# Work shared out anew between ScalarE and VectorE, and four expert lists loaded into other buffers, in a two-layer convolution and expert kernel

## The reference, cut to what matters

```python
# layer 0: grouped convolution, then a mixture of experts
c0 = conv(x, weight(32, 8, 9), groups=4, padding=4) + ctx[:, :, None] + bias[None, :, None]
logits = c0 @ W_gate + b_gate                        # 8 experts
_, top_idx = top_k(logits, 2)                        # 2 experts for each of the 4096 rows
x = x + mean_of_2(relu(c0 @ W_e[top] + b_e[top]))
# layer 1: convolution kernels mixed by attention, then an int4 product
att = softmax(gelu(gelu(cond @ W0 + b0) @ W1 + b1) @ W2 + b2)
c1 = einsum('boi,bih->boh', einsum('bk,koi->boi', att, weight), x) + (att @ bias_k)[:, :, None]
x = x + (c1 @ dequant(qweight, scales, zeros) + bias)
```

## Time and profile before

| | us |
|---|---|
| median of 3 runs | 516.99 (516.94 to 518.96) |
| the profiled execution's own time | 518.35 |
| its span in the profile | 516.6 |
| TensorE busy in that span | 491.2 (95%) |
| VectorE busy | 345.6 (67%) |
| ScalarE busy | 197.6 (38%) |

### The profile page before, as it was taken

One profiled execution on the slowest core, in us unless ns is written; L12 is line 12 of the kernel. 1 busy time (PEld: TensorE's weight loads), 2 busy tenths in 40 slices (PEclk: granted clock), 3 DMA queues, 4 the chain that ended last, 5 costly groups with the idle time before them and its releaser, 6 DMA issues. The chain is left out here.

```text
span 516.6 us, 10152 instructions
## 1 busy us (share of the span) xinstructions
PE 491.2 (95%) x2284; PEld 321.6 (62%) x2285; DVE 345.6 (67%) x1087; ACT 197.6 (38%) x341; POOL 157.5 (30%) x178
## 2 busy tenths in 40 slices
PE   5999999999869999999999999999997999999996
PEld 5999999989844443444444444444544777777674
DVE  6877888877546657573354435453445799999996
ACT  6798999999721111111111111111222222222220
POOL 9154555444435522233323332333224000000000
PEclk9999999999969999999999999999997999999998
DMA  6569878998467686676666657575554688889852
GB/s 182 142 233 298 285 241 269 361 374 269 154 165 188 209 228 168 165 201 181 174 187 163 183 150 197 163 191 146 155 143 169 245 292 292 277 292 287 286 184 102
DMA packets 90050, 110.94 MB, mean 215 GB/s; under 512 B 25198, under 2 KB 61726, under 8 KB 88980
## 3 DMA queue, kind: packets, MB, share of 16 engines
q1 hardware_dynamic: 71808, 69.14, 47.1%
q0 software_dynamic: 11664, 36.24, 19.7%
q10 hardware_dynamic: 6536, 5.09, 3.3%
HBM read 65.44 MB, written 46.51 MB: 217 GB/s over the span
## 5 line engine op out<-in xcount | busy, mean ns | idle before, releaser
L1213 PE MATMUL bank<-we,lT 128*128 x536 | 233.7, 597 | 0.7 <-DVE ring_a L953 0.7
L1213 PEld LDWEIGHTS bank<-we,lT 128*128 128x128 f32 x536 | 101.8, 191 | 128.1 <-issue 127.9
L539 POOL DMA_INDIRECT pairs_d<-ring_b,pair_i x71 | 71.0, 999 | 161.0 <-DVE pair_i L942 109.2
L630 ACT ACTIVATE ring_b<-ring_a 128x512 f32<-128x512 f32 x71 | 44.7, 630 | 196.3 <-DVE ring_a L953 188.2
L953 DVE TENSOR_TENSOR ring_a<-bank,be_bc 128x512 f32<-128x512 f32 x71 | 49.0, 691 | 101.8 <-PE bank L1213 92.4
L1187 PE MATMUL bank<-wconv,phases 128*128 128x128 f32 x768 | 93.8, 280 | 1.2 <-ACT phases L367 1.2
L522 POOL DMA_INDIRECT lists_d<-token_list,row_i x64 | 66.7, 1042 | 83.3 <-ACT token_list L596 57.1
L1187 PEld LDWEIGHTS bank<-wconv,phases 128*128 128x128 f32 x768 | 90.8, 196 | 1.4 <-ACT phases L367 1.4
L367 ACT COPY phases<-xt 32x512 f32<-32x512 f32 x64 | 71.4, 1116 | 1.2
L939 DVE STREAM_TRANSPOSE lT<-xt 128x512 f32<-128x512 f32 x71 | 49.9, 703 | 11.1 <-DMA keys<-lists_d 10.8
L367 DVE COPY phases<-xt 32x512 f32<-32x512 f32 x64 | 44.7, 698 | 10.2 <-PE bank L1187 8.5
(11 more groups left out here) (196 smaller groups left out, 384.3 us busy)
## 6 DMA issues: line engine op xcount, KB each, us to landing
xt<-lists_d SPq DMA_DIRECT2D x284, 64.0 KB, 2.1
xt<-in_x SPq DMA_DIRECT2D x60, 256.0 KB, 3.9
we<-pairs_d SPq DMA_DIRECT2D x28, 512.0 KB, 4.8
we<-in_L_ffn_W_e SPq DMA_DIRECT2D x8, 1024.0 KB, 6.5
out<-orow_list SPq DMA_DIRECT2D x32, 256.0 KB, 2.8
lists_d<-orow_list SPq DMA_DIRECT2D x8, 257.0 KB
be_bc<-in_L_ffn_b_e ACTq DMA_DIRECT2D x4, 512.0 KB, 9.5
words<-pairs_d POOLq DMA_DIRECT2D x4, 512.0 KB, 5.3
```

The costliest lines, as they stand in the source:

```text
L539: pool.indirect_dma_start(pairs_d, bass.IndirectOffsetOnAxis(ap=pair_i[:, s % DR:s % DR + 1], axis=0), ring_b[:, s % U, :], None, bounds_c ...
L630: act.activation(ring_b[:, j, :], ring_a[:, j % 2, :], ACT.Relu, scale=0.5).then_inc(result_ready, 1)
L1213: mm = pe.matmul(ps_exp[j % 2][:, :], lT[:, j, p * P:(p + 1) * P], we[:, bass.ds(expert, 1), p, :].rearrange("m a n -> m (a n)"), start=(p ...
```

## The change

There are four edits.

1. Phase 2 is copied by ScalarE for the groups with an even number only. For the odd ones it is copied by VectorE (`split_third`), at the end of the step, behind `chosen`; `dve_split` is then counted by that copy. For group 1 it stands right behind the two other copies at the start.
2. The lists of slots 0 to 3 are loaded into `ring_a[0]`, `ring_a[1]`, `ring_b[2]` and `ring_b[3]` and not into `xt`, and no longer wait for the last x to be copied. Slot 4, the first in `xt`, waits for that now.
3. The three products for the mixing kernels stand in front of `gate_and_rows` of group 31, not behind `count_ranks` of group 31.
4. `warm_up` is called twice more at the start: four transposes in front of those of the convolution's weights, and eight behind them.

```diff
@@ -121,6 +121,7 @@
         token_list = sb("token_list", [P, U, LK])
         htok = token_list[:, :, 0:L]
         ring_b = sb("ring_b", [P, U, L])
+        first_list = [ring_a[:, 0, :], ring_a[:, 1, :], ring_b[:, 2, :], ring_b[:, 3, :]]
         orow_list = sb("orow_list", [P, 2, LK])
         orow = orow_list[:, :, 0:L]
         ident = sb("ident", [P, P])
@@ -362,6 +363,10 @@
                 ins.then_inc(taps_ready, 1)
 
 
+        def list_of(a, ja):
+
+            return first_list[a] if isinstance(a, int) and a < len(first_list) else xt[:, ja, :]
+
         def split_phase(copy, q, jq, jb):
 
             return copy(phases[q * C:(q + 1) * C, jb, :, 1:P + 1],
@@ -421,15 +426,15 @@
                     else:
                         sp.reg_load(row_reg, tab[0:1, bass.ds(a - EARLY, 1)])
                     row = sp.snap(row_reg, min_val=0, max_val=E * REGION - P)
-                    if isinstance(a, int) and a < XR:
+                    if isinstance(a, int) and a == XR:
                         sp.wait_ge(act_split, NG)
                         sp.wait_ge(dve_split, NG)
-                    else:
+                    if not isinstance(a, int) or a >= XR:
                         wait(sp, lT_ready, a - XR + 1)
                         wait(sp, pair_ready, a - XR + 1)
 
                     for mh in range(MH):
-                        sp.dma_start(xt[mh * B:(mh + 1) * B, ja, :].rearrange("r (h n) -> r h n", h=MH),
+                        sp.dma_start(list_of(a, ja)[mh * B:(mh + 1) * B, :].rearrange("r (h n) -> r h n", h=MH),
                                      lists_d[bass.ds(row, P), mh * P:(mh + 1) * P].rearrange("(h r) n -> r h n", r=B)
                                      ).then_inc(list_in[ja], 16)
                     sp.dma_start(keys[:, ja, :], lists_d[bass.ds(row, P), L:LK]).then_inc(list_in[ja], 16)
@@ -573,9 +578,9 @@
                     ja = (j + 2) % U
                     wait(act, x_in[ja], ring_count(a, ja, XR))
                     wait(act, conv_done, a - 1)
-                    for q in range(PH // 2, PH):
-                        ins = split_phase(act.copy, q, ja, j % 2)
-                    ins.then_inc(act_split, 1)
+                    if ja % 2 == 0:
+                        split_phase(act.copy, 2, ja, j % 2)
+                    split_phase(act.copy, 3, ja, j % 2).then_inc(act_split, 1)
                 b = g - 2
                 if live(b, NG):
                     jb = (j - 2) % U
@@ -700,9 +705,15 @@
 
                 wait(dve, x_in[ja], ring_count(a, ja, XR))
                 wait(dve, conv_done, a - 1)
-                for q in range(PH // 2):
-                    ins = split_phase(dve.tensor_copy, q, ja, ja % 2)
-                ins.then_inc(dve_split, 1)
+                split_phase(dve.tensor_copy, 0, ja, ja % 2)
+                ins = split_phase(dve.tensor_copy, 1, ja, ja % 2)
+                if ja % 2 == 0:
+                    ins.then_inc(dve_split, 1)
+
+            def split_third(ja):
+
+                if ja % 2 == 1:
+                    split_phase(dve.tensor_copy, 2, ja, ja % 2).then_inc(dve_split, 1)
 
             dve.memset(wfull[:, :, :], 0.0).then_inc(wfull_zero, 1)
 
@@ -777,6 +788,7 @@
                 deq_step(dve.scalar_tensor_tensor(terms_w[:, :], full_low, odd[0:RK, 0:1], full, ALU.mult, ALU.add))
 
             split_x(1, 1)
+            split_third(1)
             dve.wait_ge(consts, N_CONSTS)
 
             def context_columns():
@@ -870,6 +882,8 @@
                     wait(dve, chosen1_ready, a + 1)
                     wait(dve, rank_done, a - 3)
                     dve.scalar_tensor_tensor(chosen[:, ja, :], iota_e[:, :], e2, chosen1[:, :], ALU.is_equal, ALU.add).then_inc(chosen_ready, 1)
+                if live(g + 2, NG):
+                    split_third((j + 2) % U)
 
             n_early = [0]
 
@@ -937,7 +951,7 @@
                 wait(dve, list_in[ja], (a - ja) * (80 // XR) + 80)
                 wait(dve, exp_done, a - AHEAD + 1)
                 dve.transpose(lT[:, ja, :].rearrange("m (p h r) -> m h p r", p=PH, h=MH),
-                              xt[:, ja, :].rearrange("r (h p l) -> r h p l", h=MH, p=PH)).then_inc(lT_ready, 1)
+                              list_of(a, ja).rearrange("r (h p l) -> r h p l", h=MH, p=PH)).then_inc(lT_ready, 1)
                 wait(dve, result_out[ja], 16 * ((a - DR - ja) // U + 1))
                 dve.scalar_tensor_tensor(pair_i[:, a % DR:a % DR + 1], keys[:, ja, 1:2], slot_expert[:, a:a + 1],
                                          keys[:, ja, 0:1], ALU.not_equal, ALU.add).then_inc(pair_ready, 1)
@@ -1113,7 +1127,7 @@
             pe.wait_ge(cond_in, 32)
             pe.transpose(ps_misc[:, 0:N], cond_sb[:, :], ident[:, :]).then_inc(condT_done, 1)
             pe.transpose(ps_misc[:, N:N + C], cw_sb[:, :], ident[0:C, 0:C]).then_inc(condT_done, 1)
-
+            warm_up(WARM_START // 2)
             for t in range(SHIFTS):
                 pe.wait_ge(dve_taps, t + 1)
                 pe.wait_ge(act_taps, t + 1)
@@ -1121,6 +1135,7 @@
                     mm = pe.transpose(ps_w[t][:, p * C:(p + 1) * C],
                                       wsel[:, t * PH + p, :, :].rearrange("o q i -> o (q i)"), ident[0:C, 0:C])
                 mm.then_inc(wT_done, 1)
+            warm_up(WARM_START)
 
             def context_products():
 
@@ -1235,6 +1250,7 @@
                         mm = pe.matmul(ps_low[0][0:RK, :], ones_r[:, :], wq[:, q, :], start=(q == 0), stop=(q == 3))
                     mm.then_inc(colsum_done, 1)
 
+            mix_layers(NG + 1 - mlp_first)
             gate_and_rows(NG - 1, (NG - 1) % U)
             pe.wait_ge(early, N_EARLY)
             pe.wait_ge(we_in, 16 * E)
@@ -1242,7 +1258,6 @@
             count_ranks(NG - 2, (NG - 2) % U)
             product(1, 1)
             count_ranks(NG - 1, (NG - 1) % U)
-            mix_layers(NG + 1 - mlp_first)
             for s in range(2, 5):
                 product(s, s % U)
             pe.wait_ge(tab_ready, 1)
```

## The result

The changed kernel takes **511.34 us** (median of 4 runs, 510.92 to 512.60) against 517.19 for the kernel before beside it (4 runs, 516.94 to 518.96): a ratio of 0.988, 95% interval 0.986 to 0.991. The prediction was 508.9, with 505 to 513 as its range. The profiled execution took 511.29 us, with a span of 509.2 (before: 518.35 and 516.6).

The account below looks back on a forecast made before the run. TensorE was taken to bound stage 2, with open time around the last convolution and VectorE nearly the bound in the loop. Terms -9.1 + 2.1 - 1.7 + 0.6 = -8.1 us gave 508.9 us from the 516.99 median; range 505 to 513.

Parts of the forecast that it names:

- The lists: Convolution 31 to slot 2: without the 10.1 us queue wait, 13.84 us in place of 22.96, a gain of 9.1 us.
- The loop: Looped steps of stage 1: VectorE takes 8.42 us for two steps against 8.13, a loss of 2.1 us.
- The steps written out: Steps 24 to 28, where ScalarE also has Gelu and Exp: fewer copies there gain 1.7 us.
- So in plain steps the gain is zero: Stage 1: even groups keep two ScalarE copies, so two steps stay at 7.86 us; short odd steps only give slack.
- What I put down to the Exp: Step 27: VectorE stands 2.1 us for the Exp, which comes one copy, 1.1 us, earlier.
- The start: Ahead of convolution 1: VectorE's third copy costs 0.6 us, the added transposes nothing; convolution 1 near 16.9 us.
- Which the even ring carries on: Stage 1: the 0.6 us lost ahead of convolution 1 persists through the even groups' cycle of ScalarE and TensorE.
- The mixing products: Ahead of group 31's gate products: 2.05 us leave the front of slot 2, about 0.7 us delays the gate products.
- the cover: Ahead of group 31's gate products: TensorE waits for group 30's rows anyway (1.32 us before), hiding part of the moved products.
- Everything in stages 2 and 3 moves up as a block: Behind slot 2: all later work starts earlier by the whole 9.1 us gain, with no further change.
- The sum: Whole kernel: -9.1 + 2.1 - 1.7 + 0.6 = -8.1 us, from 518.35 to 510.2 us profiled, 508.9 against the median.
- GpSimd holds up the third copy: Rival, chance 0.05: VectorE's moved copies take 2 us in place of 0.62 beside GpSimd's scatters; slower, 540 us.

Follow-up runs that it names:

- the one without filler: The changed kernel without the added warm_up transposes at the start (edit 4 taken out): 511.48 us, ratio 0.987 to the kernel before.
- the kernel with the table sooner: The changed kernel with the last rank counts one product earlier and the later lists' table ahead of the second bias sum: 510.43 us.
- the copy late: The changed kernel with the third copy on VectorE only for odd groups from 18 on, not in the loop: 510.21 us.

## Why the prediction came out as it did

**The lists.** Right in mechanism and size (8.7 us of 9.1), and the lists alone confirm it. List 0 is asked for at 128.15, near the 127.8 of the prediction, and VectorE transposes it at 139.63 without a wait. The missing 0.4 is small change: slots 0 and 1 took 7.2 us with the rank counts between them, not 6.94, and convolution 31 with the gate products of group 30 took 3.84, not 3.68; slot 2 waited 0.18 for the bias sum, as estimated.

**The loop.** Right: 8.50 us for two steps, predicted 8.42. Leaving the copy out of the loop brings the 48.7 back.

**The steps written out.** The size was right (1.8 for 1.7), the reason was not, and so the size was luck. The step "So in plain steps the gain is zero" failed. TensorE's waits for ScalarE's `token_list` from 83 to 140 us were 2.1 us before and 3.0 with the copy taken back; they are 0.2 in the changed kernel. In either of the other two 1.0 us of them lay ahead of 109 us, in plain steps. I had taken the two steps of the earlier trace rows, which have no such wait, for all of them, though the earlier trace rows has one of 1.32 us at the end of the stage. What I put down to the Exp (2.1 us of VectorE's waiting for it) did vanish from VectorE's waits, but that was only in part TensorE's time.

**The start.** Convolution 1 came at 17.00, predicted 16.9. "Which the even ring carries on" was wrong: by convolution 5 the loss was gone (32.26 against 32.37). What took it back is open. Nor is the 0.6 us shown to be the third copy's: with the copy and no filler convolution 1 came at 16.34 in the kernel with the copy alone and at 16.85 in the one without filler, with the filler and no copy at 16.23 and 16.82.

**The mixing products.** The prediction gave them 1.35 us. With them back the 1.7 us in front of the gate products came back too, so the cover was right; the gain in the changed kernel, 1.1 by the profiles and 0.6 by the medians, is not clear of the noise. Without the lists the move costs about 1, which the prediction didn't foresee. That it needs a clock that is up when the products begin fits the rows (3.78 us for 1.98), but it isn't shown as the cause.

**Stages 2 and 3.** This is the step that failed and moved the number: "Everything in stages 2 and 3 moves up as a block." 1.7 us of the gain were lost again behind slot 2, 1.5 of them ahead of slot 11. The idle time makes up 1.2: 1.93 us in front of slots 5, 8 and 11, against 0.72 before. The chain can be read in the changed kernel's rows. In front of slot 5: the memset holds the comparison, so that the table is late, and the bias sum of slot 3 stands behind it in VectorE's program (165.03); TensorE waits 0.48. Further on: the table's cast gives list 8 its row, and SyncE asks for it at 166.58. Relative to slot 2 that is 12.0 us, as before (174.83 - 162.92 = 11.9). But the list took 8.1 us to arrive rather than 6.1:

```profile
174.69 0.71 DVE L953 STREAM_TRANSPOSE lT<-xt 128x512 f32<-128x512 f32 x1 [3.58 <-DMA keys<-lists_d]
...
176.55 0.69 DVE L967 TENSOR_TENSOR ring_a<-bank,be_bc 128x512 f32<-128x512 f32 x1 [0.63 <-PE bank L1228]
```

VectorE waits 3.58 us for the keys, the bias sum behind them ends at 177.24, and TensorE has waited 0.95 by then. The kernel with the table sooner has none of these three waits, only the 1.46 us in front of slot 4, and with the memset moved too none is left, which shows the chain as a whole. That the list was slow because the DMA engines were fuller (0.95 busy from 170 to 175 us, against 0.79 from 175 to 180 before) is only argued. The waits of this stretch were visible before as 0.7 us in front of slot 11, so the table's chain had no slack to move up with.

**The reference execution.** The sum was made against a profiled execution 1.4 us above the median, and then taken off the median whole. The changed kernel's profiled execution lies on its median (511.29 and 511.34). So 1.4 us of the difference between the profiles were that execution's own, and no gain. Where it spent them isn't shown; the 0.8 us of stage 3, whose first products ran at the lower clock (2.05 us for four, 1.17 after), are one candidate.

Put together: of the 8.1 predicted, 7.4 came in the span (7.1 in the profiled times) and 5.7 between the medians. That the span came so near was luck in part: 0.8 us less in stage 3 and 0.7 less at the start, neither foreseen, made up for most of what stage 2 lost.

Of the rivals none came true in whole. "GpSimd holds up the third copy" did not: the changed kernel's copies, grouped by form (count | busy us, mean ns), took 671 ns on average with the slow start in it, and 636 from 40 to 80 us.

```profile
L372 DVE COPY phases<-xt 32x512 f32<-32x512 f32 x80 | 53.7, 671 | 3.1 <-PE bank L1202 1.2
```

Yet its mechanism was at work one stage later, on another instruction.

## What to carry to other kernels

When a wait is removed, look for the next chain that was hidden under it, above all one that starts at a fixed point behind (a table, a first request), and lay its slack beside the gain. Two edits that touch the same wait have no prices of their own: by the medians the copy lost 3.8 us alone and was 1.1 ahead with the lists, the mixing products lost 1.0 alone and were 0.6 ahead, where neither lead is clear of the noise. Three things together gave 3.8 us more than the change itself: a table made sooner, GpSimd's memset moved out of the way of a short serial chain on VectorE, and work kept out of the steps where its engine is the bound. And a sum that is made against one profiled execution has to be taken off that execution's time, not off the median.

## What the runs showed of the hardware

**A memset on GpSimd holds some of VectorE's instructions, small ones too, until it ends.** A comparison of 128x8 lasted until the end of the memset in each profile in which it began inside it (1.27 us before, 1.73 and 2.80 in kernels shown above), and it took 0.22 us where the memset had been moved. The 32x512 copy at the start follows a memset's end as well: it ended at 15.47 before, at 15.49 in the changed kernel and at 14.97 with the copy alone, each time 0.35 us behind the end of GpSimd's memset of 128x4096 (15.12, 15.14, 14.62), though it began sooner than the memset. In the changed kernel a transpose of 128x512 (158.58, 0.71 us) and a bias sum of 128x512 with one input in PSUM (159.78, 0.69 us) ran at their usual length beside the memset. The Trainium skill (SBUF — State Buffer, Who interferes with whom) says that VectorE and GpSimd share one pair of ports, that an instruction of VectorE in a two-port mode and one of GpSimd exclude each other for the whole instruction, and that copies and `tensor_scalar` can be in such a mode. These rows agree, the comparison being a `tensor_scalar`.

**The clock fell without an idle stretch ahead.** In the kernel with the memset moved, TensorE was busy throughout 140 to 150 us, and the windows read (TensorE alone: busy, PEclk, DMA share, GB/s)

```profile
144.00:146.00 2.00, 2.00 (x7) 1.00 0.84 236
146.00:150.00 4.00, 4.00 (x14) 0.60 0.74 223
```

Slot 0 took 5.04 us. The changed kernel ran the same instructions in the same order at 1.00 and took 3.60. In both the mixing products stand ahead (1.98 us for four). Of the eight profiled kernels with the lists in the idle buffers and the mixing products in this place four kept the clock in that stretch and four lost it for 3 to 4 us. Three of the four that lost it have the copy late and so a shorter stage 1, the fourth doesn't; with one profiled execution each, the profiles don't show whether the program or the execution decides. The mean clocks of all executions point to the execution: the clock was 0.992 in the profiled one of the kernel with the memset moved (512.08 us) and 0.995 to 0.996 in its four others (508.55 to 509.87 us), and 4 us at 0.60 in 510 lower a mean by 0.003 (an estimate from these rows). Idle time ahead doesn't decide it alone either: with the mixing products back TensorE stood 1.69 us and the clock stayed at 1.00, with the lists alone it stood 1.32 and 0.35 and the clock fell to 0.50. It is worth about 1.5 us, as much as most edits here.
